# One causal filter per channel made in eight portions instead of in one piece ahead of the channel loop, with two copies given to ScalarE

## The chip, the cores and the metric

The kernel runs on one core of one Trainium2 chip. The metric is the device time of one execution in microseconds. TensorE (PE; PEld is its weight load), VectorE (DVE), ScalarE (ACT), GpSimd (POOL) and SyncE (SP) each work through their own instructions in order and wait for one another by semaphores. SP and ACT also issue DMA transfers (SPq, ACTq), POOL the indirect ones.

## What is computed

`x` is 128 samples (b) of 64 channels (h) by 1024 steps (t), float32. Four residual steps follow one another. The first convolves every channel along t with a filter K of that channel, masked to each sample's length; the other three mix through low-rank tables A, B chosen by a sample's ids, and through a 64 x 64 matrix chosen by an id:

```python
P = dtA[:, :, None] * jnp.arange(length, dtype=jnp.float32)
Cs = Cc * (jnp.exp(dtA) - 1.0) / A
K = 2.0 * jnp.einsum('hn,hnl->hl', Cs, jnp.exp(P)).real
...
y = jnp.fft.irfft(u_f * k_f, n=n)[..., :Lq]
y = y + u_m * D[:, None]
return y * mask[:, None, :]
...
x = x + _L0_cond_ref(x, itok_B_8_3872, ...)      # the convolution with K
x = x + _L1_cond_ref(x, L1_cond_A, L1_cond_B, itok_B_3_7)
x = x + _L2_cond_ref(x, L2_cond_A, L2_cond_B, itok_B_4_50)
x = x + _L3_cond_ref(x, itok_B_0_31, L3_cond_weights, L3_cond_biases)
```

## The kernel before

It has three stages, each a block at whose end all engines meet.

**Setup stage** (`setup_stage`). K is made for all channels. A step number l of a channel is split as 32 a + c, so that the exponential becomes a product of a part u in a and a part v in c. DVE computes parameters for the 64 channels (some fifty instructions of 64 columns), PE transposes them into `par`, and then tables of 64 channels x 32 columns are made: turns (an angle less its whole turns) on DVE, products for the decays on POOL, exponentials and sines on ACT (each change between the two functions has an ACT_TABLE_LOAD), products with the coefficients on DVE. 64 matmuls (L426) contract them, 32 channels into each half of a PSUM region; DVE adds D to the first element, ACT makes a float16 high copy `khl[.., 0]`, DVE the low rest. SP stores each half with four DMAs (L324) of 64-byte runs into `k_rows` and `d_rows` in memory: `d_rows` are differences of parts of K. Behind the first half SP loads the Toeplitz operands of channels 0 to 2 and then issues the second half. The setup also turns the first group of the low-rank tables and computes bias, mask and row numbers.

**Channel stage** (`channel_stage`). One turn of the body is eight channels (XU = 8, u = 0 to 7, i the number of the body, h = 8 i + u). Per channel:
- SP loads `toep` and `diff` (the Toeplitz matrices of K, 4 slots) three channels ahead, once the product of channel h - 1 is done (L153, L154), and x seven channels ahead, once the slot's result has been stored (`x1_stored`, L698).
- PE transposes x of the next channel (`turn`, 8 instructions, L161), which needs `xS_ready` of this channel, and multiplies (`convolve`, 42 instructions, L973): a low half, a high half, and a product `common` that both quarters of the high half share.
- ACT splits the transposed x into a copy `xS` (L167) and the high part `xTh` (L168), and triggers the store of the result of channel h - 2 (L819).
- DVE makes the low part `xTl` (L176), the sum `xS` (L179), its high copy `xSh` (L181) and its low part `xSl` (L183), copies the low half through the mask (L932), copies `common` out of PSUM (L935), adds it (L938) and copies the high half through the mask (L942).

Bodies 1 to 4 also join one group of the tables A and B per four channels: SP loads B and A at u = 2 and 6 (L738, L739), ACT reorders A into `by_k` at u = 0 and 4 (L837; it waits for `a_loaded`, and the next `high_x` stands behind it), PE turns B and A and joins them at u = 0, 1, 2 and 4, 5, 6 (L1018, L1026, L1034). POOL gathers a matrix per pair of samples and splits it into `iwh` and `iwl`, after DVE's `selection_rows` (L888 to L918), which DVE runs at the start of the stage; after the last group it gathers 16 x 16 products. Bodies 0, 4 and 7 are written out, 1 to 3 and 5, 6 are loops.

**Pair stage** (`pair_stage`). 64 turns over pairs of samples for the other three steps.

The order of the work is written out by hand on every engine; nothing reorders it.

## Time and profile before

| | us |
|---|---|
| median of 3 runs | 784.39 |
| lowest, highest | 782.91, 786.03 |
| the profiled execution | 783.29 |
| its span, first to last instruction | 781.5 |
| PE busy in the span | 708.0 (91%) |
| DVE busy | 624.3 (80%) |
| ACT busy | 331.2 (42%) |
| POOL busy | 393.9 (50%) |

The channel stage lasts from 76 to about 496 us, the pair stage from there to the end. A busy share is an average over the three stages; only the stretches tell what holds each.

### The profile page before, as it was taken

The page shows a single profiled execution, that of the slowest core. Times are in us where ns is not written, and L with a number is a line of the kernel's source. Part 1 is how long each engine was busy: PE and PEld are TensorE (multiplying, and loading weights), DVE is VectorE, ACT ScalarE, POOL GpSimd, SP SyncE. Part 2 cuts the span into 40 slices and gives each one's busy share as a digit, 9 for nine tenths or more (in the row PEclk, how much of TensorE's full clock was granted, in tenths as well). Part 3 has the DMA queues.
Part 4 walks back from the last instruction along what each step waited for, and adds up shares of the span by engine and source line. Part 5 has one row for each costly group of instructions (what it writes and reads, how often), then busy time and mean ns, then how long its engine had stood idle before and what let it go on. Part 6 is the DMA issues. An engine that isn't in the chain of part 4 may idle for free.

```text
span 781.5 us, 19175 instructions
## 1 busy us (share of the span) xinstructions
PE 708.0 (91%) x6688; PEld 541.4 (69%) x6688; DVE 624.3 (80%) x1124; ACT 331.2 (42%) x432; POOL 393.9 (50%) x682
## 2 busy tenths in 40 slices
PE   3044899999999999999999999589999999999997
PEld 2044677778887788887777777367777777777774
DVE  7995888887887778777877777378888888888885
ACT  2611112333133333222211122058777777777775
POOL 2420588888860000004767700177667766776672
PEclk9999999999999999999999999789999999999999
DMA  4007999999999999999999995579999999999974
GB/s 154 0 1 186 312 315 299 338 325 322 332 345 338 323 331 333 335 288 333 283 319 295 311 301 160 196 265 319 311 321 324 314 318 317 315 321 315 321 264 159
DMA packets 121319, 219.95 MB, mean 281 GB/s; under 512 B 19828, under 2 KB 79796, under 8 KB 121268
## 3 DMA queue, kind: packets, MB, share of 16 engines
q1 hardware_dynamic: 102692, 166.59, 66.3%
q10 hardware_dynamic: 9360, 33.56, 11.0%
q0 software_dynamic: 9216, 19.15, 7.7%
q8 instruction: 28, 0.46, 0.2%
q14 instruction: 23, 0.19, 0.1%
HBM read 146.35 MB, written 72.91 MB: 281 GB/s over the span
## 4 chain that ended last, share of the span: by engine, by line
PE 86%; DVE 3%; DMA 1%; ACT 1%; issue 0%; DVEq 0%; SPq 0%; ACTq 0%
PE ps L973 42%; PE ps L1261 11%; PE ps L1248 7%; PE ps L161 7%; PE ps L1294 6%; PE ps L1277 3%; PE ps L1276 3%; PE ps L1267 2%; PE ps L1034 1%; PE ps L1306 1%; PE ps L1018 1%; PE ps L1026 1%; DVE x1l L1235 1%; DMA xt<-x_rows 0%; DVE xTl L1216 0%; ACT xTh L1175 0%
## 5 line engine op out<-in xcount | busy, mean ns | idle before, releaser
L973 PE MATMUL ps<-toep,xTh 128*128 128x512 f16 (+3 forms) x1024 | 209.9, 300 | 0.0
L973 PE MATMUL ps<-toep,xTl 128*128 128x512 f16 (+3 forms) x512 | 147.0, 300 | 0.0
L783 POOL DMA_INDIRECT gnow<-g_rows,idx_g x64 | 58.8, 919 | 153.6 <-DMA g_rows<-g_out 127.4
L973 PEld LDWEIGHTS ps<-toep,xTh 128*128 128x128 f16 x1024 | 97.9, 98 | 51.1 <-issue 1.1
L1131 POOL DMA_INDIRECT asel<-a_rows,idx_a x64 | 72.2, 1129 | 77.3 <-PE ps L1277 76.2
L167 ACT ACTIVATE xS<-ps 128x256 f32<-128x256 f32 x64 | 24.4, 381 | 176.8 <-PE ps L161 176.8
L176 DVE TENSOR_TENSOR xTl<-ps,xTh 128x1024 f16<-128x1024 f32 x64 | 78.3, 1223 | 24.9 <-ACT xTh L168 24.6
L1126 POOL COPY bsel<-bt 128x256 f16 x256 | 92.7, 405 | 2.4 <-issue 1.7
L758 POOL DMA_INDIRECT wnow<-in_L_cond_weights,idx_w x64 | 62.1, 970 | 55.4 <-DVEq L920 38.4
L1216 DVE TENSOR_TENSOR xTl<-ps,xTh 128x1024 f16<-128x1024 f32 x64 | 78.3, 1224 | 12.3 <-ACT xTh L1175 9.0
L973 PE MATMUL ps<-diff,xTh 128*128 128x256 f16 x512 | 87.3, 273 | 0.0
L1175 ACT ACTIVATE xTh<-ps 128x1024 f16<-128x1024 f32 x64 | 65.3, 1021 | 21.5 <-PE ps L1248 21.5
L973 PE MATMUL ps<-diff,xTl 128*128 128x256 f16 x256 | 69.8, 273 | 0.0
L973 PEld LDWEIGHTS ps<-toep,xTl 128*128 128x128 f16 x512 | 50.2, 98 | 25.2 <-issue 0.7
L168 ACT ACTIVATE xTh<-ps 128x1024 f16<-128x1024 f32 x64 | 65.4, 1021 | 0.0
L935 DVE COPY common<-ps 128x256 f32<-128x256 f32 x64 | 26.9, 421 | 44.4 <-PE ps L973 44.4
L1294 PE MATMUL ps<-bsel,xTh 128*128 128x64 f16 x1024 | 54.0, 194 | 0.0
L1294 PEld LDWEIGHTS ps<-bsel,xTh 128*128 128x128 f16 x1024 | 52.4, 99 | 0.8
L1294 PE MATMUL ps<-bsel,xTl 128*128 128x64 f16 x512 | 52.1, 194 | 0.0
L973 PEld LDWEIGHTS ps<-diff,xTh 128*128 128x128 f16 x512 | 47.4, 98 | 4.4
L1261 PE MATMUL ps<-x1h,iwh 128*128 128x512 f16 x128 | 48.6, 380 | 1.3 <-DVE x1l L1235 1.3
L1189 ACT ACTIVATE outt<-ps,bias_t 128x1024 f32<-128x1024 f32 x32 | 35.7, 1115 | 31.4 <-PE ps L1277 31.4
(225 smaller groups left out, 1649.1 us busy)
## 6 DMA issues: line engine op xcount, KB each, us to landing
toep<-k_rows SPq DMA_DIRECT2D x64, 384.0 KB, 6.5
diff<-d_rows SPq DMA_DIRECT2D x64, 384.0 KB, 8.0
xt<-in_x SPq DMA_DIRECT2D x32, 512.0 KB, 6.3
x_rows<-xt ACTq DMA_DIRECT2D x32, 512.0 KB, 6.1
xt<-x_rows SPq DMA_DIRECT2D x32, 512.0 KB, 7.3
out_dram<-outt SPq DMA_DIRECT2D x32, 512.0 KB, 7.9
out_dram<-diff SPq DMA_DIRECT2D x32, 512.0 KB
toep<-x_rows SPq DMA_DIRECT2D x24, 512.0 KB
```

The source lines that it names most:

```text
L161: last = nc.tensor.transpose(m.turned[:, j, :], x_slot(m, u)[:, j * P:(j + 1) * P], m.ident[:])
L168: nc.scalar.activation(m.xTh[:, u % 2, :, :], m.turned, ACT.Copy).then_inc(m.xTh_ready, 1)
L176: V.tensor_tensor(m.xTl[:, u % 2, :, :], m.turned, m.xTh[:, u % 2, :, :], ALU.subtract).then_inc(m.xTl_ready, 1)
L758: gp.indirect_dma_start(m.wnow[:, v, :], None, w_src, bass.IndirectOffsetOnAxis(ap=m.idx_w[:, q:q + 1], axis=0)).then_inc(w_gathered[v], 16)
L783: gp.indirect_dma_start(m.gnow[:, v, :], None, m.g_rows, bass.IndirectOffsetOnAxis(ap=m.idx_g[0:64, q:q + 1], axis=0)).then_inc(g_gathered ...
L973: last = PE.matmul(out, xs[x_part], rhs(part), start=start and k == 0, stop=stop and k == 2)
L1126: GP.tensor_copy(m.bsel[:, u % 2, n, :, :, :].rearrange("p s j r -> p (s j r)"), table[:, bass.ds(ids[n], 1), :, :, :].rearrange("p o s j ...
L1131: gp.indirect_dma_start(m.asel[:, p % U, :], None, m.a_rows, bass.IndirectOffsetOnAxis(ap=m.idx_a[:, p:p + 1], axis=0)).then_inc(a_gathere ...
L1175: S.activation(m.xTh[:, u % 2, :, :], psT, ACT.Copy).then_inc(x1Th_ready, 1)
L1216: V.tensor_tensor(m.xTl[:, u % 2, :, :], psT, m.xTh[:, u % 2, :, :], ALU.subtract).then_inc(x1Tl_ready, 1)
L1261: PE.matmul(o, w[:, bass.ds(p, 1), :].rearrange("p o d -> p (o d)"), xp[:, u % U, cut], start=(k == 0), stop=False)
L1294: done = PE.matmul(psZ, xT[:, u % 2, j, :], m.bsel[:, u % 2, :, b, j, :], start=(j == 0 and k == 0), stop=(j == J - 1 and k == 2))
```

## The change

- The setup makes K for chunk 0 alone, eight channels (E = 8). The tables have 256 columns instead of 2048. The parameters are transposed in two halves, the first as soon as it is packed. The decays are now made by ACT alone: eight activations of 32 columns with the channel's parameter as scale (`k_decay`). POOL's products are gone. The setup also loads x of channels 0 to 6 and prepares the turns and decays of chunk 1.
- Chunk i + 1 is finished in body i: ACT does the three sines and the absolute value at u = 0 (`k_trig`), DVE combines at u = 1 and makes the tables at u = 2, PE multiplies behind channel 2 (four matmuls of 128 x 64, `k_products`), DVE adds the first element at u = 3, ACT and DVE split at u = 4, and SP stores at u = 5 with eight DMAs (`store_k`) and waits for their landing ahead of `load_toeplitz` of the next body's channel 0. Turns and decays of chunk i + 2 are made at u = 6 and 7.
- In every channel ACT makes `xSh` (`high_sum`) and copies `common` (`copy_common`); the latter stands ahead of the trigger `store_x1(h - 2)`. DVE's sum comes ahead of `xTl`.
- `selection_rows` and what was at the end of the setup (bias, ids, the low parts of the first tables) are divided over the channels of body 0 (`finish_setup`). `load_group(1)` moves from u = 0 to u = 3.
- POOL waits for four gathers with one semaphore. Bodies 5 and 6 are written out.

```diff
+def high_sum(nc, m, act, h, u):
+    act.wait_ge(m.xS_summed, h + 1)
+    nc.scalar.activation(m.xSh[:, u % 2, :, :], m.xS[:, u % 2, :, :], ACT.Copy).then_inc(m.xSh_ready, 1)
...
+def k_turns_u(nc, m, dve, k):
+    V = nc.vector
+    V.tensor_tensor(m.tu[:], over_channels(m, 1, k), over_steps(m, 1), ALU.mult).then_inc(m.k_step, 1)
+    dve.wait_ge(m.k_step, K_STEPS * k + 1)
+    V.tensor_scalar(m.rounded[:], m.tu[:], MAGIC, None, ALU.add).then_inc(m.k_step, 1)
...
+def k_decay(nc, m, k, dst, s, ready):
+    for e in range(E):
+        nc.scalar.activation(dst[:, e, :], m.step[:, s, :], ACT.Exp, scale=m.par[:, 0, bass.ds(k * E + e, 1)]).then_inc(ready, 1)
+
+def k_trig(nc, m, act, k):
+    S = nc.scalar
+    act.wait_ge(m.turns_u_ready, k + 1)
+    S.activation(m.su[:], m.tu[:], ACT.Sin, scale=-TWO_PI).then_inc(m.trig_s, 1)
+    S.activation(m.cu[:], m.tu[:], ACT.Abs).then_inc(m.abs_u_ready, 1)
+    act.wait_ge(m.abs_u_ready, k + 1)
+    S.activation(m.cu[:], m.cu[:], ACT.Sin, scale=-TWO_PI, bias=m.phase[:, 2:3]).then_inc(m.trig_c, 1)
+    act.wait_ge(m.turns_v_ready, k + 1)
+    S.activation(m.tv[:], m.tv[:], ACT.Sin, scale=-TWO_PI, bias=m.phase[:, 1:2]).then_inc(m.trig_v, 1)
...
+def store_k(m, sp, k):
+    sp.wait_ge(m.khl_ready, 2 * k + 2)
+    for e in range(2):
+        for n, rows in enumerate((m.k_rows, m.d_rows)):
+            for part in range(2):
+                dst = rows[bass.ds(k * E + e * KP, KP), part, 0:L].rearrange("q (a c) -> a q c", c=TC)
+                sp.dma_start(dst, m.khl[64 * e + 32 * n:64 * e + 32 * n + 32, part, :, :]).then_inc(m.k_stored, 16)
...
@@ channel stage, SP @@
+                            if make_k and u == XU - 3:
+                                store_k(m, sp, i + 1)
+                                sp.wait_ge(m.k_stored, 128 * (i + 2))
                             load_toeplitz(m, sp, h + 3, (u + 3) % U)
...
@@ channel stage, ACT @@
                             high_x(nc, m, u)
+                            high_sum(nc, m, act, h, u)
+                            copy_common(h - 1, first and u < 2)
                         if not (first and u < 2):
                             store_x1(h - 2, (u - 2) % XU)
+                        if make_k and u == 0:
+                            k_trig(nc, m, act, i + 1)
+                        if make_k and u == 4:
+                            act.wait_ge(m.k_stored, 128 * (i + 1))
+                            k_high(nc, m, act, i + 1, 3)
+                        if start_k and u == 6:
+                            act.wait_ge(m.tables_ready, i + 2)
+                            k_decay(nc, m, i + 2, m.dv, 0, m.decay_v_ready)
+                        if start_k and u == 7:
+                            k_decay(nc, m, i + 2, m.du, 1, m.decay_u_ready)
...
@@ channel stage, DVE @@
-                        V.tensor_copy(m.common[:], conv_common).then_inc(common_added, 1)
-                        dve.wait_ge(common_added, 2 * h + 1)
+                        if make_k and u == 1:
+                            k_combine(nc, m, dve, i + 1)
+                        if make_k and u == 2:
+                            k_tables(nc, m, dve, i + 1)
+                        if make_k and u == 3:
+                            k_first(nc, m, dve, i + 1, 3)
+                        if make_k and u == 4:
+                            k_low(nc, m, dve, i + 1, 3)
+                        if start_k and u == 6:
+                            k_turns_u(nc, m, dve, i + 2)
+                        if start_k and u == 7:
+                            k_turns_v(nc, m, dve, i + 2)
+                        if first:
+                            finish_setup(u)
```

ACT at the start of body 4, which is written out in both kernels (`outt` is `by_k`); before:

```order
L167 ACTIVATE xS<-ps 128x256
L168 ACTIVATE xTh<-ps 128x1024
L819 DMA x_rows<-x1l 128x1024
L837 ACTIVATE outt<-outt 128x1024
L167 ACTIVATE xS<-ps 128x256
```

and in the changed kernel:

```order
L193 ACTIVATE xS<-ps 128x256
L194 ACTIVATE xTh<-ps 128x1024
L200 ACTIVATE xSh<-xS 128x256
L851 ACTIVATE common<-ps 128x256
L844 DMA x_rows<-x1l 128x1024
L262 ACT_TABLE_LOAD
L262 ACTIVATE k_su<-k_tu 128x256
L263 ACTIVATE k_cu<-k_tu 128x256
L265 ACTIVATE k_cu<-k_cu,phase 128x256
L267 ACTIVATE k_tv<-k_tv,phase 128x256
L884 ACTIVATE outt<-outt 128x1024
L193 ACTIVATE xS<-ps 128x256
```

The store of the result stands behind the copy of `common`, and the sine block behind the store, ahead of the reordering of A and of the next channel's copies.

SP in the second half of the same body, from the load of x at u = 4 to the group's next tables or their place; before:

```order
L698 DMA xt<-in_x 128x1024
L153 DMA toep<-k_rows 128x2x768
L154 DMA diff<-d_rows 128x4x384
L698 DMA x1h<-in_x 128x1024
L153 DMA toep<-k_rows 128x2x768
L154 DMA diff<-d_rows 128x4x384
```

and in the changed kernel:

```order
L725 DMA xt<-in_x 128x1024
L344 DMA k_rows<-khl 32x4x32 x2
L344 DMA d_rows<-khl 32x4x32 x2
L344 DMA k_rows<-khl 32x4x32 x2
L344 DMA d_rows<-khl 32x4x32 x2
L179 DMA toep<-k_rows 128x2x768
L180 DMA diff<-d_rows 128x4x384
L725 DMA x1h<-in_x 128x1024
```

Eight stores of K, and the wait for their landing, stand ahead of the Toeplitz load of the next body's first channel.

DVE in body 0 between the masked copies of channel 6; before:

```order
L932 COPY_PREDICATED x1l<-mask,ps 128x512
L935 COPY common<-ps 128x256
L938 TENSOR_TENSOR ps<-ps,common 128x512
L942 COPY_PREDICATED x1l<-mask,ps 128x512
L176 TENSOR_TENSOR xTl<-ps,xTh 128x1024
```

and in the changed kernel the first of the rows put in (six more pairs like the last follow, of which four write `idx_a` and `idx_g`, and then the addition):

```order
L1009 COPY_PREDICATED x1l<-mask,ps 128x512
L232 TENSOR_TENSOR k_tu<-par,step 128x256
L234 TENSOR_SCALAR k_rounded<-k_tu 128x256
L236 SCALAR_TENSOR_TENSOR k_tu<-k_rounded,k_tu 128x256
L975 TENSOR_SCALAR tmp<-idf,row_cols 32x64
L976 TENSOR_SCALAR tmp<-idf,row_cols 32x64
L975 TENSOR_SCALAR tmp<-idf,row_cols 32x64
L976 TENSOR_SCALAR tmp<-idf,row_cols 32x64
```

The copy of `common` is gone from DVE, and three operations of K and sixteen of the row numbers stand ahead of the addition and of the next channel's low part.

## Rows read from the trace of the kernel before

**Rows 1.** The page: busy tenths in 40 slices of 19.5 us.

```profile
PE   3044899999999999999999999589999999999997
...
DVE  7995888887887778777877777378888888888885
```

**Rows 2.** Chain of waits, pieces in order: start us, us, what.

```profile
138.61 5.22 PE ps L973 x42
...
171.32 0.87 PE ps L1026 x8
...
185.73 0.87 PE ps L161 x8
...
192.70 1.08 PE ps L161 x8
```

**Rows 3.** One stretch: us; busy PE, PEld, DVE, ACT, POOL; clock; DMA share; GB/s.

```profile
165.00:192.00 27.00, 27.00 (x238) 21.52 (x237) 22.18 (x31) 8.25 (x12) 23.06 (x24) 1.00 0.98 327
```

**Rows 4.** Timeline of ACT and SP around 166 to 188 us: start us, us, what.

```profile
166.64 0.34 ACTq L819 DMA_DIRECT2D x_rows<-x1h  x1
...
174.70 0.35 SPq L698 DMA_DIRECT2D x1h<-in_x  x1
...
188.01 1.06 ACT L837 ACTIVATE outt<-outt 128x1024 f32<-128x1024 f32 x1 [6.09 <-DMA outt<-in_L_cond_A]
```

**Rows 5.** Timeline: the packed parameters are transposed.

```profile
16.70 0.69 PE L415 MATMUL ps<-ident,packed 64*128 64x64 f32 x4 [3.68 <-DVEq L533]
```

**Rows 6.** Timeline: K's products, its stores, the first Toeplitz load, the stage's start.

```profile
49.83 10.45 PE L426 MATMUL ps<-iwh,bt 128*64 128x32 f32 x100 [30.55 <-DVEq L579]
...
59.39 0.95 SPq L324 DMA_DIRECT2D k_rows<-khl  x2
60.39 1.19 SPq L324 DMA_DIRECT2D d_rows<-khl  x2
63.83 0.40 SPq L153 DMA_DIRECT2D toep<-k_rows  x1
...
71.90 3.79 SPq L324 DMA_DIRECT2D d_rows<-khl  x2
...
76.28 1.94 PE L161 MATMUL ps<-ident,xt 128*128 128x128 f32 x8 [5.55 <-PEq L297]
```

**Rows 7.** Timeline of DVE: operations of 256 columns.

```profile
372.99 0.46 DVE L181 CAST xSh<-xS 128x256 f16<-128x256 f32 x1
...
375.30 0.42 DVE L935 COPY common<-ps 128x256 f32<-128x256 f32 x1 [0.53 <-PE ps L973]
...
379.09 0.29 DVE L181 CAST xSh<-xS 128x256 f16<-128x256 f32 x1
```

**Rows 8.** Chain of waits: first and last of the sixteen index rows.

```profile
77.30 0.30 DVE tmp L901
...
81.35 0.20 DVE idx_g L907
```

**Rows 9.** Timeline: small operations and a table load of ACT; one DVE operation twice.

```profile
9.22 0.26 ACT L367 ACTIVATE work<-work 64x64 f32<-64x64 f32 x1 [7.19 <-DVE work L501]
9.38 0.24 ACT L368 ACTIVATE work<-work 64x64 f32<-64x64 f32 x1
24.79 5.60 DVE L545 SCALAR_TENSOR_TENSOR iwh<-x1l,iwh 128x2048 f32<-128x2048 f32 x1
32.24 1.89 ACT L383 ACTIVATE iwl<-iwl 128x2048 f32<-128x2048 f32 x1
33.88 2.29 DVE L548 SCALAR_TENSOR_TENSOR iwh<-bt,iwh 128x2048 f32<-128x2048 f32 x1
34.15 1.28 ACT L385 ACT_TABLE_LOAD   x1
35.44 1.91 ACT L385 ACTIVATE x1h<-iwh 128x2048 f32<-128x2048 f32 x1
```

**Rows 10.** DMA issues by target: engine, count, KB each, median us to landing.

```profile
d_rows<-khl SPq DMA_DIRECT2D x4, 64.0 KB, 3.1
```

More of the change, by code:

```diff
@@ L176, in low_x @@
     V.tensor_tensor(m.xTl[:, u % 2, :, :], m.turned, m.xTh[:, u % 2, :, :], ALU.subtract).then_inc(m.xTl_ready, 1)
[L177 to L183 removed]
+    dve.wait_ge(m.xS_summed, h + 1)
```

531 lines of the change are left out of this document (284 added, 247 removed).

## Prediction

> **What bounds the kernel now.** I read three views in this order: the page's forty slices, the chain of waits, and the timeline around the change of stage. The slices [rows 1] show three parts: until about 88 us PE is mostly empty while DVE is full; then PE is at 9 until about 496 us (the channel stage); then the pair stage, which this change does not touch. In the channel stage the chain [rows 2] is PE's alone: 5.22 us of products and 0.87 us of transposes, with their gaps 6.10 us a channel, and group work between. So a saving in the setup counts in full, and anything that makes PE wait in the channel stage is lost in full. Two further things are nearly full there. The sixteen DMA engines have a share of 0.98 while groups are made [rows 3]. And ACT's copy `by_k`, which waits for a table of A, has its data 2.3 us into the period that began at 185.73 us; the next turn on PE is 0.2 us longer than usual (1.08 against 0.87) [rows 2, 4]. There is no slack left at that place.
>
> **The setup.** Unchanged until the parameters are packed (16.6 us) [rows 5]. Today 32 channels of tables follow on every engine, then the stores, and the stage cannot start until SP has issued the second half of K at 75.69; PE's first transposes stand at 76.28 [rows 6]. Afterwards chunk 0 has 256 columns per operation, and 256-column operations of DVE take 0.29 to 0.46 us [rows 7]. Seven for the turns 2.9 (with waits), the copy of `par` 0.25, five small ones 0.9, three to combine 1.3, four for the tables 1.5: 23.5. The four matmuls: 100 records of the old ones took 10.45 us, two records a matmul, so 0.21 us each [rows 6] and 0.85 for four: 24.4. First element, ACT's two high copies and DVE's two low ones 1.6: 26.0. Eight stores at the 0.54 us that the first four took, 4.3, and 2.25 us from the last issue to the next load [rows 6]: 32.6. Six loads and the store of `a_rows`, 4.2, and 0.55 of block change: the stage starts at 37.4 instead of 76.28, **-38.9**. What the setup drops elsewhere (POOL's products, 100 records on PE) lies under this path; ACT's exponentials come from the early half of the parameters (about 10 us) and are done long before DVE needs them.
>
> **The first nine channels.** Before, from 76.28 to the start of channel 9's products at 138.61 is 62.3 us [rows 2, 6]; DVE's selection rows, with 4.3 us of index rows among them [rows 8], sat in front of the second channel. After, counted from the stage's start: channel 0 is done at 7.8; DVE has a piece of setup in between, so PE's `a1_back` starts at 8.7, and channel 1's products at 10.45. From there eight channels at 6.10 and one group transpose make 49.7. DVE's extra work in front of what PE waits for: the last table and `a1_low` in channel 2 are late by 2.7, the product of K itself 0.85, the biases 0.3, turns and the sixteen index rows in channels 6 and 7 4.0, the sine block at channel 8 0.8. That is 8.7, so channel 9 starts at 68.9 or 69.0: **+6.7** against before.
>
> **From channel 9 to the end of the stage** there are chunks 2 to 7 to make, in bodies 1 to 6 of eight channels.
> - PE: 6 x 0.85 = 5.1.
> - DVE loses the copy `common` (0.42) and the conversion `xSh` (0.29 to 0.46) of every channel [rows 7] and gets a chunk of about 14 operations and two small pairs per eight channels, 5.9 us: even. Its chain from the end of ACT's high copy to `xSl` falls from about 2.6 to 2.1 us. Only in bodies 5 and 6, where no group work covers it, the tables are 0.65 late for PE: 1.3.
> - ACT gets 0.8 us per channel, hidden, and two table switches per chunk. A load takes 1.28 us; the exponentials are 8 instructions that start 0.16 apart or a bit more [rows 9]. PE's next transposes need `xSl`, 3.5 us after `high_x` starts. The sine block (1.28 + 4 x 0.38 and waits, about 2.9) moves `high_x` from 0.95 to 3.7 and, with `by_k` behind it, 4.5 us into the period. The limit is 3.45 with a group: 1.05 lost. Without a group it is 2.6: 1.1 lost. At bodies 5 and 6 this is 2.2, the exponentials of body 5 another 1.1; in group bodies the transpose and join cover them.
> - The store of x1 now waits behind `copy_common`, that is for the next channel's products: about 4.9 us later (it was triggered 4.7 us ahead of them, [rows 2, 4]). SP waits for it before each load of x, and behind that stand the Toeplitz loads and the group's tables. With an unchanged landing time the A table would be 4.9 late at channels 4; but DMA queues are then shorter (the landing of that store was 8.0 us, [rows 4], under a share of 0.98), so I take 0.8 at each of four places: 3.2. The bounds are 0 and 4.9.
> - The eight stores of a chunk and the wait for their landing stand in SP's queue in front of `load_toeplitz` for the next body's channel 0, and behind that its channels 1 and 2, two loads of x, and the next group's tables. Issue 4.3, landing 3.1 [rows 10], from about 7 us after channel 4: the Toeplitz load goes at about 15 and lands at 21 to 22.5; it is needed at 22.3 with a group, 19.2 (and 1 of other stalls) without. I take 0.5 for four bodies and 1.3 for two: 4.6. The A table for the next body arrives at about 3.7 of the period instead of 2.3, behind the sine block; together with it 2.0 at each of three boundaries: 6.0.
> Sum: 5.1 + 1.3 + 2.2 + 1.1 + 3.2 + 4.6 + 6.0 = **+23.5**.
>
> **The sum.** 781.5 - 38.9 + 6.7 + 23.5 = 772.8 of span; the profiled execution was 1.8 us longer than its span (783.29), so 774.6. The median of the three runs is 784.39, the lowest 782.91. Half a per cent is about what can be told from no change: below 780.5 is faster, above 788.3 slower.
>
> **A rule against this change.** The table load at 34.15 starts 0.02 us after the previous activation ends and the next activation starts at its end: 1.28 us and nothing more [rows 9]. The Trainium skill, ScalarE: Activation LUTs, section What ACT_TABLE_LOAD costs, adds a drain of about 1.38 us to every switch, 2.66 in all. By the rows the sum stays as above; by the rule the estimate would grow by 1.38 at each of some eight exposed switches, to about 785.6.
>
> **Rivals.**
> - *Everything on DMA hides* (the shorter chain on DVE and shorter queues absorb it): the 3.2 and 4.6 vanish and the three boundaries cost only the 1.05 of the sine block: 774.6 - 3.2 - 4.6 - 2.85 = 764. For it: 5% less load per microsecond as soon as PE stalls a little. Against: a share of 0.98 [rows 3].
> - *SP's queue becomes the bound; slower.* In the second half of K the four stores took 7.5 us to issue, 1.9 each, because Toeplitz loads filled the queue [rows 6]. If the eight take even half that, 0.95 each, every chunk comes 3.3 us later, and SP has no slack behind it; together with tables late by the upper bound at channels 4 (4 x 4.1 = 16.4 more), the sum is 774.6 + 6 x 3.3 = 794 with the stores alone and 811 with both. It decides from 1.0 us more at each of ten places (six chunks, four group tables), where the gain is used up. For it: the DMA share of 0.98. Against: at that point of the body SP has just waited for a landing, so that its queue is short, and each store is an eighth as large.
> - *ACT is longer than I say; slower.* If each table switch costs another 1.4 us at eight exposed places, whatever its cause (a pipeline emptied in front of it, register reads between the eight exponentials in a loop), 774.6 + 11 = 786. For it: the exponentials take their scale from a column in memory, of which no row shows the price. Against: the switch in the setup [rows 9].
> - *The setup saves less*: seven loads of x are queued ahead of K's stores. They are 3.7 MB, issued by 20 us; at the 300 GB/s of the stage [rows 3] they have landed by 26. If not, 3 us more: 778.
> - *DVE shares its memory port with POOL*: the same operation took 5.60 us beside a POOL product and 2.29 without [rows 9]. POOL makes `iwh` and `iwl` in bodies 1 to 3. If each of DVE's memory-only K operations doubled there, 10 us would be added to DVE's work and some 4 of them to PE: 779.
>
> **How the numbers follow.** Main case with its small variants (setup, port) 0.50, range 766 to 782; all hidden 0.17, 764; SP's queue 0.20, 785 to 811; ACT 0.10, 786; elsewhere 0.03. I forecast 774.6. To leave out no more than 2 in 10, from 762 to 792. Faster takes most of the main case and all of the second, 0.65; within half a per cent a bit of the main case and most of ACT's, 0.15; slower 0.20.
>
> **What would show it.** The first transposes of the channel stage at 36 to 39 us; channel 9 some 30 to 34 us earlier than at 138.61; in the chain of the stage the products of K with 0.85 a chunk. In ACT's rows a table load of 1.28 with nothing around it. PE idle ahead of the first Toeplitz product of a body: the stores of K. PE idle ahead of transposes: `xSl`, and by it ACT's sine block or the A table. The landing of the A table relative to the period's start tells the third and fourth item. The prediction is wrong if PE's waits between channel 9 and the stage's end sum to less than 8 or more than 30 us, or if the pair stage (283 us) changes by more than 2.

## The result, and the profile after

| | before | changed |
|---|---|---|
| median of 7 runs (us) | 784.39 | 792.43 |
| lowest and highest | 782.91, 786.03 | 788.91, 803.28 |
| span of the profiled execution | 781.5 | 790.6 |
| ratio to before, 95% interval | 1 | 1.0094 (1.0071 to 1.0117) |

The changed kernel is 0.9% slower; an execution more than 1.5% above the fastest of its kernel is left out of ratios and intervals (803.28 here, five of the ten of e10_before_copies). The forecast of 774.6 was wrong in its sign, and the median lies just outside the range of 762 to 792. The profiled execution took 792.43 us, 9.1 more than the one of before (783.29), and that is what has to be explained.

The page of the changed kernel, slices of 19.8 us, then shares of the chain of waits:

```profile
PE   2299899969979997999999999579999999999997
...
PEclk9599999989999998999999999889999999999999
...
PE 67%; DMA 11%; DVE 6%; SPq 4%; issue 4%; ACT 3%; POOL 0%; POOLq 0%; ACTq 0%; DVEq 0%
```

Against [rows 1] the empty start of PE is half as long: PE fills from the third slice on instead of the fifth. But in the stretch in which PE had only nines there are now a 6 and two 7s, three or four slices apart, and the granted clock has an 8 at two of those places. The chain, which was PE's alone in the channel stage [rows 2], has 11% of DMA and 4% of SP's queue in it.

The chain in order, from the start of the stage to channel 9 and then around the change from the second to the third body of eight channels (start us, us, what):

```profile
37.20 1.94 PE ps L187 x8
...
105.82 0.87 PE ps L187 x8
106.70 5.22 PE ps L1061 x42
...
133.56 7.06 DMA x_rows<-xt
...
143.59 0.79 SPq L344
...
145.91 4.53 DMA d_rows<-khl
...
153.83 0.65 SPq L765
154.68 10.71 DMA outt<-in_L_cond_A
...
169.23 1.16 DVE xSl L213
170.44 1.97 PE ps L187 x8
172.41 6.93 PE ps L1061 x42
```

The stage starts at 37.20 (37.4 was predicted) and channel 9's products at 106.70 (106.3 or 106.4 was predicted, 138.61 before [rows 2]). Up to there the change does what was forecast: 32 us are gained. Then comes a chain that did not exist before and that can be read line by line: the landing of an x1 store (L844, `x_rows<-xt`), SP's load of x which waits for it, the eight stores of K (L344), their landing (`d_rows<-khl`, 4.53 us), the Toeplitz loads, the B table (L765), the A table with 10.71 us, and only then ACT and DVE and PE's transposes.

What each piece costs PE can be taken from the starts of the 63 sets of transposes in the timeline. The table gives the time that the periods between two starts are longer than before, by place. Body 1 to 4 run from the tenth to the 42nd start (219.2 us before). "Boundary" are the two periods at the change of body, three times; "channel 4" and "behind K" (the period with K's product on PE) occur four times each. What is left of bodies 1 to 4 (1.4 us in the changed kernel, up to 3.8 in the others, 5.3 in e10) is mostly in a period behind a late one; in the changed kernel 0.8 of it is body 5's sine block in the last period. Each row is one execution. Where its time is more than 2 us from the median, the two are: e1_store_first 777.02 (median 772.57), e2_group_ahead 781.51 (787.60), e3_both 771.95 (769.88), e4_copies_on_dve 782.70 (780.41), e6_four_stores 785.20 (787.70), e8_no_switch 769.24 (766.54), e10_before_copies 801.57 (797.25).

| kernel | 1st start | 10th start | boundaries | channel 4 | behind K | bodies 1 to 4 | after the 42nd | 63rd start |
|---|---|---|---|---|---|---|---|---|
| before | 76.3 | 137.6 | 0 | 0 | 0 | 0 | 0 | 484.9 |
| changed | 37.2 | 105.7 | 24.3 | 5.7 | 3.9 | 35.3 | 4.7 | 492.9 |
| e1_store_first | 37.3 | 105.7 | 10.4 | 2.4 | 4.7 | 18.2 | 4.6 | 475.8 |
| e2_group_ahead | 37.3 | 106.8 | 4.2 | 8.6 | 5.4 | 21.4 | 5.7 | 481.2 |
| e6_four_stores | 36.4 | 105.8 | 12.8 | 7.7 | 6.0 | 28.6 | 4.9 | 486.7 |
| e12_no_stores | 37.0 | 106.4 | 3.7 | 11.4 | 5.7 | 24.6 | 4.7 | 483.0 |
| e4_copies_on_dve | 37.0 | 105.2 | 7.4 | 0.8 | 13.6 | 24.5 | 3.8 | 480.7 |
| e3_both | 37.4 | 105.5 | 2.5 | 3.3 | 5.6 | 12.3 | 4.5 | 469.7 |
| e8_no_switch | 37.7 | 103.4 | 9.5 | 2.4 | 4.5 | 16.4 | 2.7 | 469.8 |
| e9_store_low_four | 35.8 | 103.8 | 6.3 | 0.0 | 4.6 | 11.7 | 4.5 | 467.3 |
| e7_all | 35.9 | 104.1 | 2.8 | 0.0 | 5.8 | 11.0 | 4.7 | 467.2 |
| e10_before_copies | 77.1 | 136.1 | 1.4 | 12.9 | 0 | 19.6 | 0.0 | 502.9 |
| e11_before_copies_store_first | 77.1 | 136.1 | 0.3 | 0.0 | 0 | 0.3 | 0.0 | 483.7 |

In the changed kernel 31.9 us are gained by the tenth start, 40.0 are lost from there to the 63rd (35.3 + 4.7; 23.5 was predicted), and 1.0 behind it. Of the 40.0, 24.3 are at the three boundaries: 17.2 in the first of the two periods, where PE waits, and 7.1 in the second, where PE is busy without a gap at a granted clock of 0.72 to 0.76. Of the 387.28 us from the tenth start to the 63rd PE is idle for 24.0, in the kernel before for none of 347.30.

Two long stretches, bodies 1 to 4 of the kernel before and of the changed one (us; busy PE, PEld, DVE, ACT, POOL; granted clock; share of the DMA engines; GB/s):

```profile
138.00:357.00 219.00, 219.00 (x1912) 174.88 (x1911) 174.18 (x271) 65.42 (x95) 77.99 (x82) 1.00 0.99 328
```

```profile
106.00:360.00 254.00, 232.11 (x1943) 182.10 (x1941) 175.60 (x276) 122.93 (x255) 121.21 (x125) 0.96 0.87 283
```

Before, PE was busy for all of the 219.00 us; now it is idle for 21.9 of 254, and the clock is lower. ACT has nearly twice the work, and still less than half of the time.

One boundary in the timeline of the changed kernel, ACT and PE (start us, us, engine, line; in brackets the idle time before it and what ended it):

```profile
157.07 0.38 ACT L851 ACTIVATE common<-ps 128x256 f32<-128x256 f32 x1 [2.09 <-PE ps L1061]
...
157.71 1.28 ACT L262 ACT_TABLE_LOAD   x1 [0.26 <-issue]
159.00 0.42 ACT L262 ACTIVATE k_su<-k_tu 128x256 f32<-128x256 f32 x1
...
160.22 0.51 ACT L267 ACTIVATE k_tv<-k_tv,phase 128x256 f32<-128x256 f32 x1
165.41 1.06 ACT L884 ACTIVATE outt<-outt 128x1024 f32<-128x1024 f32 x1 [4.68 <-DMA outt<-in_L_cond_A]
...
156.87 1.04 PE L187 MATMUL ps<-ident,xt 128*128 128x128 f32 x8
...
170.44 1.97 PE L187 MATMUL ps<-ident,xt 128*128 128x128 f32 x8 [5.20 <-DVE xSl L213]
```

The period begins at 156.87. The sine block is over at 160.73, 3.9 us into it, as forecast (3.7). But the A table lands at 165.39, 8.5 us into the period; before it was 2.3 [rows 2, 4]. ACT's `by_k` (L884) stands ahead of the next channel's high copies, so `xSl` and with it PE wait: 5.20 us of idle time.

What made the table late was decided half a body earlier. When the store of x1 (channel 11) is triggered, in the changed kernel:

```profile
129.99 1.02 ACT L194 ACTIVATE xTh<-ps 128x1024 f16<-128x1024 f32 x1
131.58 0.42 ACT L200 ACTIVATE xSh<-xS 128x256 f16<-128x256 f32 x1 [0.57 <-DVE xS L209]
133.37 0.38 ACT L851 ACTIVATE common<-ps 128x256 f32<-128x256 f32 x1 [1.38 <-PE ps L1061]
133.56 0.39 ACTq L844 DMA_DIRECT2D x_rows<-xt  x1
```

The trigger goes 3.57 us after the start of `xTh`, and at the three channels ahead of this one 5.0 to 5.4 us after it. In the kernel before the same store went 1.10 us after the start of `xTh`:

```profile
159.44 1.02 ACT L168 ACTIVATE xTh<-ps 128x1024 f16<-128x1024 f32 x1
160.54 0.34 ACTq L819 DMA_DIRECT2D x_rows<-xt  x1
```

Counted from the start of its period, the trigger moved from 2.5 us (158.08 to 160.54) to 6.5 us (127.07 to 133.56). The next store, at 166.64 [rows 4], stood 0.09 us behind the start of its `xTh` (166.55); now it stands 4.99 us behind it (137.58 to 142.57).

Three theories were put to the test. **A**: the late trigger of the x1 store. **B**: K's stores and the wait for their landing, in SP's queue ahead of the Toeplitz loads and the group's tables. **C**: ACT's additional work, with its table loads.

### The profile page after: what moved, and what is told of

The parts are those of the page before. It is cut to its first block, busy times and chain, and to the rows that moved or that the text cites. A ratio compares the mean times of both kernels' runs of the same rounds, so it can differ in the third digit from the quotient of the medians.

```text
span 790.6 us, 19415 instructions
## 1 busy us (share of the span) xinstructions
PE 713.4 (90%) x6624; PEld 539.0 (68%) x6624; DVE 578.4 (73%) x1109; ACT 431.3 (55%) x743; POOL 380.8 (48%) x679
## 4 chain that ended last, share of the span: by engine, by line
PE 67%; DMA 11%; DVE 6%; SPq 4%; issue 4%; ACT 3%; POOL 0%; POOLq 0%; ACTq 0%; DVEq 0%
PE ps L1061 27%; PE ps L1382 10%; PE ps L1369 7%; DMA outt<-in_L_cond_A 5%; PE ps L1415 5%; PE ps L187 5%; PE ps L1398 3%; PE ps L1397 3%; DMA x_rows<-xt 3%; PE ps L1388 2%; SPq L344 1%; DMA d_rows<-khl 1%; PE ps L1427 1%; ACT xTh L194 1%; PE ps L308 1%
## 5 line engine op out<-in xcount | busy, mean ns | idle before, releaser
L1061 PE MATMUL ps<-toep,xTh 128*128 128x512 f16 (+3 forms) x1024 | 214.8, 306 | 0.6 <-issue 0.6
L1061 PE MATMUL ps<-toep,xTl 128*128 128x512 f16 (+3 forms) x512 | 149.5, 305 | 0.0
L851 ACT ACTIVATE common<-ps 128x256 f32<-128x256 f32 x64 | 24.5, 383 | 151.5 <-PE ps L1061 151.2
L1027 DVE TENSOR_TENSOR ps<-ps,common 128x512 f32<-128x512 f32 x64 | 44.6, 698 | 49.9 <-ACT common L851 49.6
L209 DVE TENSOR_TENSOR xS<-ps,xS 128x256 f32<-128x256 f32 x64 | 27.0, 422 | 69.8 <-ACT xTh L194 69.5
L1296 ACT ACTIVATE xTh<-ps 128x1024 f16<-128x1024 f32 x64 | 65.4, 1022 | 12.2 <-PE ps L1369 12.1
L187 PE MATMUL ps<-ident,xt 128*128 128x128 f32 x256 | 38.8, 301 | 31.3 <-DVE xSl L213 20.5
L187 PEld LDWEIGHTS ps<-ident,xt 128*128 128x128 f32 x256 | 32.3, 155 | 33.9 <-issue 19.2
```

Source lines behind the costliest of these rows:

```text
L187: last = nc.tensor.transpose(m.turned[:, j, :], x_slot(m, u)[:, j * P:(j + 1) * P], m.ident[:])
L1061: last = PE.matmul(out, xs[x_part], rhs(part), start=start and k == 0, stop=stop and k == 2)
L1296: S.activation(m.xTh[:, u % 2, :, :], psT, ACT.Copy).then_inc(x1Th_ready, 1)
```

## The experiments

Each change is against the changed kernel unless another is named. Ratios are against runs of the kernel before on the same chip; the medians of before in these batches were 785.36, 784.07 and 784.81 us.

**e1_store_first**: the x1 store is triggered directly behind `high_x`.

```diff
                             high_x(nc, m, u)
-                            high_sum(nc, m, act, h, u)
-                            copy_common(h - 1, first and u < 2)
                         if not (first and u < 2):
                             store_x1(h - 2, (u - 2) % XU)
+                        if not (first and u == 0):
+                            high_sum(nc, m, act, h, u)
+                            copy_common(h - 1, first and u < 2)
```

> The changed kernel with one thing of ACT's order undone: the trigger of the store of x1 (channel h - 2) stands directly behind high_x again, ahead of high_sum and copy_common. Everything else as changed (792.4 us). Theory A (SP's queue is late because x1 is stored 4.9 us later, so that the loads of x, the stores of K and the tables of A behind them all come later): the A table at the starts of bodies 2, 3 and 4 arrives about 4.9 us earlier, the waits of ACT for it (4.7 us each) vanish, PE keeps its clock there, and each of the three boundaries, 9.2 us longer than before now, costs 1 to 2: 792.4 - 23 = about 769. Theory B (the stores of K and their landing alone hold SP; the load of x in front of them is not what they wait for): no more than 5 us less, 787 or more. Theory C (ACT's sine block delays high_x): unchanged, 791 to 794.

Measured: 772.57 us (5 runs, 770.96 to 777.02), ratio 0.983 (0.979 to 0.986). That is 19.9 us less than the changed kernel by medians, and 15.4 less between the two profiled spans (790.6 and 775.2). The order of three instructions on ACT decides the sign of the whole change. ACT of this kernel at the same boundary:

```profile
129.51 0.34 ACTq L844 DMA_DIRECT2D x_rows<-xt  x1
129.52 1.02 ACT L194 ACTIVATE xTh<-ps 128x1024 f16<-128x1024 f32 x1
...
155.77 1.28 ACT L262 ACT_TABLE_LOAD   x1
...
159.74 1.06 ACT L885 ACTIVATE outt<-outt 128x1024 f32<-128x1024 f32 x1 [1.02 <-DMA outt<-in_L_cond_A]
```

The trigger stands beside `xTh` again. The period begins at 155.16, the A table is there 4.6 us into it instead of 8.5, and `by_k` waits 1.02 us instead of 4.68. The links between move with it: counted from the 14th start, SP's load of x goes at 0.9 us (135.51) instead of 4.7 (140.78), and the A table is issued 5.2 us ahead of the boundary's period (149.93) instead of 2.2 (154.68). At the boundaries 13.9 us are saved, at the channels 4 3.3.

**e2_group_ahead**: the order of the changed kernel on ACT, but SP loads the second group's B and A tables ahead of K's stores.

```diff
+                            if next_group and u == XU - 3:
+                                sp.wait_ge(b_turned, 2 * i)
+                                sp.wait_ge(a_ordered, 2 * i)
+                                load_group(2 * i + 1)
                             if make_k and u == XU - 3:
                                 store_k(m, sp, i + 1)
...
-                            if next_group or u < U:
+                            if u < U:
```

> The changed kernel with the second load_group of a body (B and A of the next body's first group) issued at u = 5 ahead of the stores of K, instead of at u = 6 behind them; same waits for its buffers. Theory A/B (the A table comes late because it stands behind the stores of K and their landing, 9.8 us from the first issue to the next Toeplitz load): ACT's wait for A at the boundaries is gone (3 x 4.7 and the half clock behind it), but the Toeplitz operands of the next body's channel 0, which land just in time now, come 3 to 4 us later behind 1 MB more: boundaries fall from 9.2 to about 5, 792.4 - 12 = about 780. Theory C (the sine block): unchanged, 791 to 794.

Measured: 787.60 us (10 runs, 781.51 to 793.16), ratio 1.004 (1.001 to 1.007). The boundaries fall from 24.3 to 4.2 in its profiled execution, which was the shortest of its ten, but the channels 4 rise to 8.6. So the tables are late at the boundary because they stand behind K's stores; once they don't, ACT waits for the other table of the group instead (1.72 and 1.60 us at the last two channels 4, 0.30 and 0.46 in the changed kernel). At the first boundary PE waits 1.81 us for `diff`, which now stands behind the group's tables. The runs spread over 11.7 us, and the median is 7.6 above the 780 that was expected.

**e4_copies_on_dve**: `xSh` and `common` are made by DVE again.

```diff
-    act.wait_ge(m.xS_summed, h + 1)
-    nc.scalar.activation(m.xSh[:, u % 2, :, :], m.xS[:, u % 2, :, :], ACT.Copy).then_inc(m.xSh_ready, 1)
...
+    V.tensor_copy(m.xSh[:, u % 2, :, :], both).then_inc(m.xSh_ready, 1)
...
+                        V.tensor_copy(m.common[:], conv_common).then_inc(common_copied, 1)
```

> The changed kernel with the second part of the change undone: xSh and the copy of common are DVE's again, ACT makes neither; the trigger of the store stands behind high_x as in the kernel before. Theory A: as with the store first, the boundaries shrink: about 769 to 774, with up to 5 us for DVE's longer chain ahead of PE's transposes. Theory B: 787 or more. If the copies on ACT were worth something by themselves, this kernel is slower than the one with the store first by that much: by the chain (0.5 us later xSl at some 12 places where DVE is late) 3 to 6 us.

Measured: 780.41 us (7 runs, 779.48 to 782.70), ratio 0.994 (0.992 to 0.996). This kernel has no late store either, since nothing stands ahead of it on ACT, and so it is to be compared with e1_store_first: 7.8 us slower, where 3 to 6 were expected. The place is new, 13.6 us behind K. PE at the first of the four, after 123 us:

```profile
123.71 1.91 PE L308 MATMUL ps<-k_tv,u_all 128*128 128x64 f32 x8 [3.67 <-DVE k_tv L296]
125.42 1.91 PE L187 MATMUL ps<-ident,x1h 128*128 128x128 f32 x8
```

K's product waits 3.67 us for the last table, which DVE makes too late with the copies in its list. So the two copies on ACT are worth their place, 7.8 us, as long as nobody waits for what stands behind them.

**e6_four_stores**: `khl` lies with its two parts inside, so that four DMAs of 16 KB store a chunk instead of eight of 8 KB.

```diff
-            for part in range(2):
-                dst = rows[bass.ds(k * E + e * KP, KP), part, 0:L].rearrange("q (a c) -> a q c", c=TC)
-                sp.dma_start(dst, m.khl[64 * e + 32 * n:64 * e + 32 * n + 32, part, :, :]).then_inc(m.k_stored, 16)
+            dst = rows.rearrange("h s z -> (h s) z")[bass.ds(2 * (k * E + e * KP), 2 * KP), 0:L].rearrange("q (a c) -> a q c", c=TC)
+            sp.dma_start(dst, m.khl[64 * e + 32 * n:64 * e + 32 * n + 32, :, :, :].rearrange("p q s c -> p (q s) c")).then_inc(m.k_stored, 16)
```

> The changed kernel with four stores of K per chunk instead of eight (both parts in one DMA, the tile khl laid out so), the same bytes in the same 64-byte runs. Theory B (SP's issue of the stores, 4.9 us, and the landing): SP is 2 to 2.5 us earlier at every boundary, and 3 boundaries get 2.5 us shorter and a bit of the half clock back: 792.4 - 9 = about 783; the setup 2 us shorter: 781. Theory A as the only cause: the setup's 2 us alone, about 790. Theory C: 790.

Measured: 787.70 us (10 runs, 784.17 to 792.86), ratio 1.004 (1.001 to 1.007), 4.7 less than the changed kernel by medians. The four issues fewer shorten the same chain, but it stays a chain: 12.8 us at the boundaries, of which 7.8 at the last one. The expected 781 was missed by 6.7.

**e12_no_stores**: from chunk 1 on K isn't stored, there is no landing to wait for, and the Toeplitz loads take the rows of chunk 0 for every channel (the output is not the reference's).

```diff
                             if make_k and u == XU - 3:
-                                store_k(m, sp, i + 1)
-                                sp.wait_ge(m.k_stored, 128 * (i + 2))
-                            load_toeplitz(m, sp, h + 3, (u + 3) % U)
+                                sp.wait_ge(m.khl_ready, 2 * (i + 2))
+                            load_toeplitz(m, sp, (u + 3) % XU, (u + 3) % U)
...
-                            act.wait_ge(m.k_stored, 128 * (i + 1))
```

> The changed kernel with the store of x1 late as it is, and the stores of K inside the channel stage and the wait for their landing left out; every channel's Toeplitz operands are read from the rows of chunk 0, same shapes and bytes, so that the output is not the reference's. This prices the stores of K in SP's queue by themselves. If the late store of x1 alone explains the A table (theory A pure): still 785 or more. If the stores of K alone do (theory B): 792.4 - 25 = about 767. If each is harmless without the other, since both lengthen the same chain on SP, this kernel and the one with the store first (772.6) come out alike, and their gains (20 and about 25) do not add up.

Measured: 784.76 us (10 runs, 782.78 to 787.12), ratio 0.999 (0.997 to 1.001), 7.7 less than the changed kernel. All of K's storing in the channel stage, taken away, brings less than half of what moving one trigger brings, and the two kernels do not come out alike, as they would if the late trigger were harmless without the stores: this one is 12.2 us above e1_store_first. It is a gain at the boundaries (3.7 instead of 24.3) and a loss at the channels 4 (11.4 instead of 5.7), with 2.4 more in the periods behind them and 1.8 behind K. Here, as in e2_group_ahead, ACT waits for the table of the channels 4 instead (0.49, 1.76, 0.68 and 2.18 us). How that reaches PE is told below (`khl`).

**e10_before_copies** and **e11_before_copies_store_first** ask the same of the kernel before: nothing of K's chunks, the setup as it was, the two copies on ACT, and DVE's sum ahead of `xTl` as in the change. The first has the change's order, the second the store ahead.

```diff
                             high_x(nc, m, u)
+                        if not (first and u == 0):
+                            high_sum(nc, m, act, h, u)
+                            copy_common(h - 1, first and u < 2)
                         if not (first and u < 2):
                             store_x1(h - 2, (u - 2) % XU)
```

```diff
                             high_x(nc, m, u)
                         if not (first and u < 2):
                             store_x1(h - 2, (u - 2) % XU)
+                        if not (first and u == 0):
+                            high_sum(nc, m, act, h, u)
+                            copy_common(h - 1, first and u < 2)
```

> The kernel before, with the second part of the change alone: xSh and the copy of common on ACT, in the order of the change (the store of x1 behind copy_common). K is still made in the setup. Theory A (the later store holds SP and with it the A tables): in the kernel before, ACT's wait for A leaves PE no slack at u = 0 and u = 4 of bodies 1 to 4, so a store 4.9 us later costs 2 to 5 us at each of seven places, and the half clock where it is more than 3: 784 + 14 to 35, about 800. If the delay of the store hurts only together with the stores of K in SP's queue: 782 to 786.

> The same with the trigger of the store ahead of the two copies, as in the kernel before. Theory A: the loss is gone, 782 to 785; the copies by themselves save nothing where PE is the bound, except at the seven waits for A, where DVE's chain is 0.5 us shorter.

Measured: the first had ten runs from 786.77 to 801.83 us with a median of 797.25, 1.6% above the 784.81 of the kernel before. The ratio of 1.009 (1.006 to 1.012) is that of the five shortest; the profile is one of the five near 800 us, so that its rows are an upper reading. The second took 784.58 us (10 runs, 781.61 to 786.20), ratio 0.999 (0.997 to 1.000). So the copies on ACT gain nothing by themselves in a kernel without K's work on DVE, and the late trigger costs at least 0.9% in a kernel that has no chunk of K at all. In that profile the cost stands at the channels 4 (6.0, 4.2, 1.5 and 1.2 us) and in the periods behind the first two (2.7 and 2.5). ACT and PE there:

```profile
164.17 1.06 ACT L854 ACTIVATE outt<-outt 128x1024 f32<-128x1024 f32 x1 [7.02 <-DMA outt<-in_L_cond_A]
...
169.50 1.97 PE L162 MATMUL ps<-ident,x1l 128*128 128x128 f32 x8 [5.80 <-DVE xSl L189]
```

The waits of ACT for the A table sum to 24.3 us here (7 of them, the longest 7.0) and to 5.6 in the second (4, 2.6). In the kernel before they were 29.2 (7, 6.1), and hidden, because ACT had nothing else to do: a sum of waits does not tell what they cost PE. What does is the line in which PE itself waits for `xSl`: 13.9 us (6, 5.8) in the first, 1.0 in the second, 2.1 before.

**e3_both** puts e1 and e2 together (both edits as above, against the changed kernel).

```diff
                             high_x(nc, m, u)
+                        if not (first and u < 2):
+                            store_x1(h - 2, (u - 2) % XU)
...
+                            if next_group and u == XU - 3:
...
+                                load_group(2 * i + 1)
```

> The store of x1 first and the group's tables ahead of the stores of K, together; base is the kernel with the store first alone (772.6 us). If what is left at the boundaries there (1.9, 3.8 and 4.8 us) is the A table, which still lands 0.6 to 2 us after ACT could take it, it goes: 772.6 - 5 = about 768, if the Toeplitz operands of the next body's channel 0, now 4 us later, stay in time. If those become late, as they did where the group's tables alone were moved (turns of 9.7 and 9.8 us where 7.0 are usual), it is 772 to 778.

Measured: 769.88 us (4 runs, 767.56 to 771.95), ratio 0.981 (0.978 to 0.983), 2.7 us below e1_store_first. The boundaries are down to 2.5 us, in place of the 6.0 that the prediction allowed.

**e8_no_switch** is e1_store_first with Identity instead of Exp in the decays, so that the sine table stays loaded (the output is not the reference's).

```diff
-        nc.scalar.activation(dst[:, e, :], m.step[:, s, :], ACT.Exp, scale=m.par[:, 0, bass.ds(k * E + e, 1)]).then_inc(ready, 1)
+        nc.scalar.activation(dst[:, e, :], m.step[:, s, :], ACT.Identity, scale=m.par[:, 0, bass.ds(k * E + e, 1)]).then_inc(ready, 1)
```

> The kernel with the store first, and the decays made with Identity in place of the exponential, so that ACT needs one table load in the whole program instead of 13; K and with it the output are not the reference's. Nothing else changes. Theory C (each of the exposed switches costs its 1.28 us, or 2.66 with a drain): at the bodies' starts the sine block is 1.3 shorter; six places of u = 0 and about two of u = 6. With the rows' 1.28: 772.6 - 6 to 10 = about 765; with a drain of another 1.4 each: about 755. If the switches are covered: 771 or more.

Measured: 766.54 us (4 runs, 765.70 to 769.24), ratio 0.977 (0.975 to 0.979), 6.0 us below e1_store_first. Groups by line of e1_store_first, then of this kernel (busy us, mean ns):

```profile
L255 ACT ACT_TABLE_LOAD x8 | 10.3, 1283 | 0.1
L262 ACT ACT_TABLE_LOAD x8 | 10.3, 1283 | 3.8 <-PEq L423 3.7
L476 ACT ACT_TABLE_LOAD x1 | 1.3, 1283 | 0.8 <-PEq L1460 0.8
```

```profile
L476 ACT ACT_TABLE_LOAD x1 | 1.3, 1283 | 0.8 <-PEq L1460 0.8
```

Sixteen loads of 1.283 us are gone, 20.5 us of ACT's time, and 6.0 us of the kernel's. In the table 2.3 of them are ahead of the tenth start and 1.9 behind the 42nd, where no group work covers ACT. Theory C is real and small.

**e9_store_low_four** is e1_store_first with four stores as in e6, and `k_low` at the start of channel 4 instead of behind the channel's work on DVE. This is aimed at a wait that the prediction had not listed (below).

```diff
                         xt = x_slot(m, u)
+                        if make_k and u == 4:
+                            k_low(nc, m, dve, i + 1, 3)
                         if not (last and u == XU - 1):
                             low_x(nc, m, dve, h + 1, u + 1)
...
-                        if make_k and u == 4:
-                            k_low(nc, m, dve, i + 1, 3)
```

> The kernel with the store first, with DVE's low copies of K at the start of u = 4 (ahead of low_x instead of behind the masked copy, so that PE's turn_b of that channel does not wait for them) and with four stores of K per chunk. The wait of turn_b was 2.05 us at each of four places in the changed kernel, but 0.6 at most with the store first; the stores' issue 4.9 us becomes 2.5. Expected 772.6 - 1.5 - 3 x 2 - 1.5 (setup) = about 763; if SP's issue is not what holds the A table, 769 or more.

Measured: 768.88 us (4 runs, 768.00 to 770.45), ratio 0.981 (0.978 to 0.983), 3.7 below e1_store_first, and 5.9 above the 763 that was expected. The channels 4 are at zero.

**e7_all** is e9 with the second group's tables ahead of K's stores, as in e2.

```diff
+                            if next_group and u == XU - 3:
+                                sp.wait_ge(b_turned, 2 * i)
+                                sp.wait_ge(a_ordered, 2 * i)
+                                load_group(2 * i + 1)
...
-                            if next_group or u < U:
+                            if u < U:
```

> All four: store first, the group's tables ahead of the stores of K, the early low copies, four stores. If Toeplitz operands and A table both come in time, what is left over the kernel with none of PE's waits is the sine block and K's products: about 760. If the Toeplitz operands are late behind the group's 1 MB, it is no better than the same without the group's tables ahead.

Measured: 766.72 us (4 runs, 766.09 to 767.94), ratio 0.977 (0.975 to 0.980). This is the best of the kernels that compute all of the reference's output: 2.3% faster than the kernel before and 25.7 us faster than the changed one, and its runs lie within 1.9 us. The expected 760 was missed by 6.7. ACT and the load at the same boundary:

```profile
155.02 0.42 ACT L262 ACTIVATE k_su<-k_tu 128x256 f32<-128x256 f32 x1
...
156.19 0.49 ACT L267 ACTIVATE k_tv<-k_tv,phase 128x256 f32<-128x256 f32 x1
156.59 1.04 ACT L888 ACTIVATE outt<-outt 128x1024 f32<-128x1024 f32 x1
```

`by_k` now follows the sine block without any wait. What is left in its stage are PE's waits for `xSl`, 8.0 us in 8 pieces, the longest 2.9 (3.6 of it ahead of the tenth start), waits for K's tables (2.6 us behind the tenth start) and K's matmuls.

## Why the prediction was wrong

- **The setup: right.** The stage starts at 37.20; 37.4 was forecast. The sum of DVE's 256-column operations, the four matmuls, the eight stores and the first loads holds. The rival of loads queued ahead of K's stores (3 us) did not occur.
- **The first nine channels: right.** Tenth start 31.9 us earlier; the two terms made 32.2.
- **PE's matmuls for K: right in size.** The periods with K's product cost 0.9 where nothing else is late (three of the four in bodies 1 to 4, the other 1.2; 1.4 in bodies 5 and 6, with the tables); 0.85 was taken.
- **Bodies 5 and 6: too dear.** There is 4.7 us behind the 42nd start and 0.8 in the period ahead of it, 5.5 in all, of which K's product is 1.7. The sines cost 0.8 at each of two, the exponentials 1.0 and the tables 0.5 at each of two: 3.6 where 4.6 was allowed. What was too much is the Toeplitz load behind K's stores (2.6 in these bodies, 4.6 in all): no row of the changed kernel's waits between 106 and 497 us has PE waiting for `toep` or `diff`. The chain of the stores was seen, and its first victim was named wrongly: it was not the Toeplitz load, but the A table behind it in the same queue.
- **The later x1 store: the step that failed.** Its term was 3.2 us, at the channels 4 alone, with the reason that "DMA queues are then shorter". The trigger is later as described (3.57 us behind `xTh`, and 5.0 to 5.4 at the three channels ahead). Its landing did not get shorter: SP's load of x went 7.40 us behind the trigger in the kernel before (160.54 to 167.94) and 7.22 now (133.56 to 140.78). With the trigger moved back the channels 4 cost 3.3 less, which is the size of the term by luck, since PE waits there for another step (`khl`, below); the boundaries cost 13.9 less. Its cost in the kernel before without any of K's chunks is 12.9 at the channels 4 by the upper reading of e10, with ACT waiting up to 7.0 us for a table, and 7 us by its ratio. The share of the DMA engines did fall, from 0.98 [rows 3] to 0.87 between 106 and 360 us, but it was 1.04 at the boundary itself (157 to 163 us), so I take the fall for a consequence of the waits, not a cure for them. And the lateness was not carried on to the boundary: there the A table was to arrive "at about 3.7 of the period". It was there at 8.5, 8.5 and 7.6.
- **The boundaries: 24.3 instead of 6.0.** The term of 2.0 each took the landing of the K stores and the sine block, but added neither the late x1 store to the chain of SP's queue nor what PE's clock does behind a wait of 5 us (7.1 of the 24.3; last section). e1_store_first takes 13.9 of it away and e12_no_stores 20.6; together that is more than there is, because the two lie in one chain: SP's load of x waits for the landing of x1, K's stores wait behind the load, and the table waits behind K's stores. That the channels 4 get dearer when the boundaries get cheaper (5.7 to 8.6 and 11.4 in e2 and e12) I read so: a boundary at which PE waits gives the queues time to catch up. The first channel 4, which lies ahead of any boundary, differs little (2.3 us in e12, 2.0 in the changed kernel), the second does (4.6 and 1.0). No run was made for that.
- **Not listed: PE's wait for `khl`.** At channel 4 the group's turn of B (L1108) needs the bank that `k_low` releases, and `k_low` stands behind the low parts of the next channel in DVE's list, which wait for ACT. DVE and PE at the first channel 4 of the changed kernel:

```profile
132.59 1.39 DVE L213 TENSOR_TENSOR xSl<-xS,xSh 128x256 f16<-128x256 f32 x1
...
134.51 0.59 DVE L333 TENSOR_TENSOR khl<-ps,khl 64x128 f16<-64x128 f32 x2
...
135.16 1.09 PE L1108 MATMUL ps<-ident,bsel 128*128 128x128 f32 x8 [1.83 <-DVE khl L333]
```

  All of PE's idle time at the channels 4 of these kernels is this wait, and none is for `xSl`: 4.8 us in four pieces in the changed kernel, 1.5 in e1, 7.4 in e2, 6.9 in e6, 9.7 in e12, none in e9 and e7. So what holds ACT there reaches PE by this step, which the prediction did not have. `k_low` was moved only together with the earlier trigger; what it brings with the late one, no run shows.
- **The sign that was set** (wrong if PE's waits behind channel 9 sum to less than 8 or more than 30 us) did not show: they sum to 24.0. The other 16.0 of the 40.0 are time in which PE is busy, 363.24 us instead of 347.30, among it some 5.6 of K's products and the 7.1 at the lower clock. A sign that counts waits alone does not see the clock.
- **The rivals.** *SP's queue becomes the bound* was right in the sign, and its second part (tables late by the upper bound at the channels 4) is close to the true mechanism, but not in its price for the stores: eight of them took 5.5 us to issue (141.41 to 146.94), 0.69 each, not 0.95, and without any stores the kernel is still 12.2 us above e1. *ACT is longer than I say* fell: 16 table loads less gave 6.0 us, 0.4 each. *DVE shares its memory port with POOL* is seen on single rows (below): `xSl` is 1.39 us instead of a median of 0.42 at the first channel 4 and 1.15 at the first boundary, both times on the way to PE's wait.

The rule that was weighed did not decide anything. The load at 157.71 lasts 1.28 us, and the sine begins at 159.00; the activation ahead of it ended 0.26 us before the load. The Trainium skill, ScalarE: Activation LUTs, section What ACT_TABLE_LOAD costs, adds a drain to that; no row here shows one, and its 1.38 us more for each of the sixteen, an estimate by that page of 22.1 us of ACT's time, has no place to stand in. The same section of the Trainium skill gives the price that the prediction found in no row, an activation that takes its scale from a column in memory. One of the two groups of them in the changed kernel, from 37 to 500 us:

```profile
L255 ACT ACTIVATE k_du<-step,par 128x32 f32<-128x32 f32 x48 | 10.8, 307 | 0.9 <-issue 0.7
```

They take 307 ns each, and eight of them took 1.80 us at 149.95, so that they start about 0.21 apart (1.80 less 0.31, by seven). By the figures of that section of the Trainium skill (186 ns, 93 more for an operand that is a column, 0.833 for each element, 93 of overlap between two) an estimate for 32 columns is 306 ns, and 213 between starts; the trace agrees.

## What to carry to other kernels

A DMA trigger in an engine's queue is work like any other: before an instruction with a wait is placed ahead of it, follow what the landing releases, over the whole chain and not only the next instruction. Where three landings stand one behind the other in one queue (a store, the stores behind it, the load behind those), their delays add, and the victim is the last one; sum the chain once, instead of giving each link a term with its own slack. A stage in which PE is busy 219.00 of 219 us and the DMA engines 0.99 has no slack for such a chain, and its runs spread where PE waits on it (e2, e6 and e10 by 8.7 to 15.1 us, e7 by 1.9).

## What the runs showed of the hardware

- **PE's clock after a pause.** Stretches of the changed kernel around the boundary (us; busy PE, PEld, DVE, ACT, POOL; granted clock; share of the DMA engines; GB/s):

```profile
157.00:163.00 6.00, 6.00 (x51) 4.49 (x49) 4.42 (x6) 3.36 (x6) 5.32 (x6) 1.00 1.04 363
...
170.40:179.30 8.90, 8.86 (x52) 6.40 (x53) 8.47 (x11) 1.72 (x3) 7.67 (x8) 0.70 0.86 293
```

  Behind the idle time of 5.20 us the granted clock is 0.70 in the mean of 8.9 us, that is, part of the time at 1.2 GHz instead of 2.4: eight transposes take 1.97 us instead of 1.04, and 42 products 6.93 instead of 5.22. In e1_store_first PE pauses 1.74, 1.99 and 2.95 us at the three boundaries; behind the first the clock stayed at 1.00 (164.03 to 171.06 us), behind the other two it was 0.80 in the period that followed, which is 1.7 us longer than before each time. So shorter pauses can cost it too, and not every time: in e4_copies_on_dve it stayed at 1.00 behind a pause of 2.06 us (234.53 to 241.56). The 3 us that the expectation of e10_before_copies set for the lower clock is not what these rows show. In the changed kernel the pause of 5.20 us costs a further 0.9 + 1.7 = 2.6 us in the next period, which the prediction's terms did not have; the second periods of the boundaries are 9.6, 9.1 and 9.3 instead of 7.0 long.
- **DVE beside POOL.** The same subtraction `xSl` of 128x256 takes 0.41 to 1.39 us, 0.42 in the median of 64:

```profile
168.95 1.15 POOL L804 TENSOR_TENSOR iwl<-wboth,iwh 128x512 f16<-128x512 f32 x1
...
169.23 1.15 DVE L213 TENSOR_TENSOR xSl<-xS,xSh 128x256 f16<-128x256 f32 x1
...
192.66 0.47 DVE L213 TENSOR_TENSOR xSl<-xS,xSh 128x256 f16<-128x256 f32 x1
```

  The long one lies beside a POOL subtraction until 170.10, and the step is the last one ahead of PE's transposes; the one of 1.39 at 132.59 lies beside the same POOL instruction (132.54, 1.15 us). That it is a shared port was only read from such rows; no run took POOL's work away.
